# A dynamic-convolution block on one core: a new order of the first three images' work, a shorter coefficient chain, and the moments' gather one group earlier

## The reference, cut to what matters

```python
x0 = (x - mean) / sqrt(var + 1e-5)              # _gn: per image and channel
pooled = x0.mean(axis=(-2, -1))
gate = softmax(pooled @ gate_w.T + gate_b)      # (16, 7)
kw1 = einsum('be,eoihw->boihw', gate, experts_w1) + conv1_w   # kb1, kw2, kb2 likewise
out1 = relu(conv3x3_same(x0, kw1) + kb1)        # per image
out2 = conv3x3_same(out1, kw2) + kb2
result = x + x0 + out2
```

## Time and profile before

| | us |
|---|---|
| median of three runs | 357.04 |
| profiled execution | 357.09 |
| its span | 355.1 |
| TensorE busy | 308.5 |
| VectorE busy | 269.6 |
| ScalarE busy | 254.0 |
| GpSimd busy | 204.7 |

### The profile page before, as it was taken

One profiled execution on the slowest core, in us unless ns is written; L12 is line 12 of the kernel. 1 busy time (PEld: TensorE's weight loads), 2 busy tenths in 40 slices (PEclk: granted clock), 3 DMA queues, 4 the chain that ended last, 5 costly groups with the idle time before them and its releaser, 6 DMA issues.

```text
span 355.1 us, 7776 instructions
## 1 busy us (share of the span) xinstructions
PE 308.5 (87%) x3047; PEld 218.8 (62%) x3047; DVE 269.6 (76%) x571; ACT 254.0 (72%) x294; POOL 204.7 (58%) x240
## 2 busy tenths in 40 slices
PE   1416955499999998999899999999999989999994
PEld 2315743257767686777677677766776867655552
DVE  3699955588969798798879897989697978693432
ACT  1155229896969797898879797979697968866710
POOL 8038607593939485676749493949294947921000
PEclk9999969699999999999999999999999999999999
DMA  8942940599999799979998999999998993665055
GB/s 196 223 76 60 223 95 3 109 201 205 202 207 219 176 213 213 212 169 209 217 210 167 210 208 211 183 209 207 218 185 187 216 217 79 166 141 144 2 134 133
DMA packets 109380, 60.87 MB, mean 171 GB/s; under 512 B 102944, under 2 KB 105248, under 8 KB 109344
## 3 DMA queue, kind: packets, MB, share of 16 engines
q1 hardware_dynamic: 108544, 59.79, 80.8%
q10 hardware_dynamic: 608, 0.59, 0.6%
q0 software_dynamic: 192, 0.01, 0.0%
HBM read 19.47 MB, written 18.87 MB: 108 GB/s over the span
## 4 chain that ended last, share of the span: by engine, by line
PE 66%; DVE 18%; DMA 8%; ACT 3%; issue 3%; SPq 1%; ACTq 0%; DVEq 0%
PE pg L381 63%; DVE mix L649 7%; DMA wts<-wts 7%; DVE a L679 2%; DVE col L658 2%; PE pg L340 2%; DVE stats L607 2%; DMA natural<-in_L_conv_conv_w 1%; DVE wts L665 1%; SPq L297 1%; DVE wts L672 1%; PE pstat L361 1%; ACT xh L496 1%; ACT c L549 1%; ACT a L501 1%
## 5 line engine op out<-in xcount | busy, mean ns | idle before, releaser
L381 PE MATMUL pg<-a,wts 128*64 128x480 f16 (+1 forms) x1440 | 291.9, 363 | 11.5 <-DMA wts<-wts 6.1
L381 PE MATMUL pg<-c,wts 128*64 128x480 f16 (+1 forms) x1440 | 292.4, 367 | 0.0
L381 PEld LDWEIGHTS pg<-c,wts 128*64 128x64 f16 x1440 | 154.3, 110 | 49.4 <-issue 0.9
L381 PEld LDWEIGHTS pg<-a,wts 128*64 128x64 f16 x1440 | 155.0, 110 | 46.6 <-DMA wts<-wts 8.5
L539 ACT ACTIVATE hid<-pg,col 128x480 f32<-128x480 f32 x80 | 52.6, 658 | 45.2 <-PE pg L381 36.7
L869 POOL TENSOR_TENSOR a<-xh,a 128x576 f16<-128x576 f32 x64 | 79.0, 1271 | 4.4 <-issue 2.1
L549 ACT COPY c<-a 64x2352 f32<-64x2352 f32 (+2 forms) x48 | 71.9, 1497 | 2.3 <-DVE a L679 1.9
L850 POOL TENSOR_TENSOR col<-col,minus_half 128x1 f32<-128x1 f32 x16 | 13.8, 860 | 99.5 <-DVE col L622 99.5
L679 DVE TENSOR_TENSOR a<-hid,a 128x480 f16<-128x480 f32 x80 | 53.1, 665 | 22.6 <-ACT a L539 22.4
L649 DVE SCALAR_TENSOR_TENSOR mix<-bank,gate,mix 128x386 f32<-128x386 f32 x96 | 62.9, 655 | 2.4
L883 POOL TENSOR_SCALAR img<-img,col 128x1152 f32<-128x1152 f32 x32 | 64.6, 2025 | 0.1
(11 more groups left out here) (60 smaller groups left out, 140.9 us busy)
## 6 DMA issues: line engine op xcount, KB each, us to landing
c<-a SPq DMA_DIRECT2D x28, 588.0 KB, 6.5
img<-in_x SPq DMA_DIRECT2D x56, 288.0 KB, 7.0
out<-img SPq DMA_DIRECT2D x60, 180.0 KB, 3.1
out<-img SPq DMA_DIRECT2D x60, 108.0 KB, 2.4
wts<-wts SPq DMA_DIRECT2D x28, 96.0 KB, 3.2
c<-a SPq DMA_DIRECT2D x8, 294.0 KB, 5.2
img<-in_x SPq DMA_DIRECT2D x16, 144.0 KB, 5.0
out<-img SPq DMA_DIRECT2D x4, 120.0 KB, 2.1
```

The costliest lines, as they stand in the source:

```text
L381: last = nc.tensor.matmul(pg[g][side * 64:side * 64 + 64, at:at + nb * W].rearrange("p (b w) -> p b w", w=W), wts[s.c % WSETS][kind][:, v, ...
```

## The change

- **ScalarE** issues the loads of the first kernel set, then the six small rows (until now GpSimd's), then the second set. It copies kernel parts 0, 2, 4, 5, 6, 7, VectorE 1 and 3; parts 4 to 7 go through pg[4] and pset.
- **VectorE** takes image 0's statistics in two halves as soon as the first set is padded. mixture_first(v), weights_first(v) mix image 0's kernels by convolution, v = 0 first: seven operations on 193 columns each, then the same for v = 1 later. Image 1 and on are mixed whole. Only image 0's conv1 weights are crossed by VectorE; its conv2 weights and all of image 1's are crossed by DMA.
- **Images 0 and 1** do conv1 in two passes (early_conv1: HI with two products, LO with the third), with the normalised image made, lowered and crossed in halves. Gathers and logits of images 1 to 3 stand between these passes, and the orders of all engines are written out up to image 3's gather; slot starts at 2 (1 on GpSimd), with image 1's conv1 ahead of image 0's conv2 as before.
- **warm_up** has 8 matmuls instead of 7, behind the gather of image 1, and doesn't wait for weights.
- **hid** has four buffers instead of two; the two new ones lie in natural.
- **coefficients** has four operations instead of six: channel_moments also writes the difference OFF of partition and channel mean, from which gwp follows in one operation; the gate's product comes ahead of the normalisation's offset.
- **In every slot** the gather stands behind conv1's third group instead of its fourth, and softmax_in behind finish(2) instead of finish(1).

The core of the diff, with long deletions left out:

```diff
 EARLY = 2
-WARM = 7
+WARM = 8
...
+            def cross_weights_first():
...
+            load_early(first)
+            load_early(second)
+            load(third)
+            cross1_early(first, HI, 0)
+            cross1_early(first, HI, 1)
+            cross1_early(first, LO, 0)
+            cross1_early(second, HI, 0)
+            cross1_early(first, LO, 1)
+            cross1_early(second, HI, 1)
+            cross_weights_first()
+            load(fourth)
+            cross1_early(second, LO, 0)
+            cross_weights(second)
+            cross1_early(second, LO, 1)
...
             def warm_up():
-                pe.wait_ge(whi_ok, 1)
+                pe.wait_ge(wt_dve, 2)
                 for _ in range(WARM):
-                    nc.tensor.matmul(pset[:, P:2 * P], ident[:, :], same[:, :], start=True, stop=True)
+                    nc.tensor.matmul(pg[3][:, 0:P], ident[:, :], same[:, :], start=True, stop=True)
...
+            def early_conv1(s, g, part):
+                if part == HI:
+                    if g == 0:
+                        if s.known(0):
+                            pe.wait_ge(w_early, 1)
+                        else:
+                            pe.wait_ge(w_crossed[s.ring], 32)
+                        pe.wait_ge(crossed1_high[s.ring][0], 32)
+                    elif g == 2:
+                        pe.wait_ge(crossed1_high[s.ring][1], 32)
+                    if s.known(0):
...
+            transpose_kernels(0)
+            transpose_kernels(1)
...
+            transpose_kernels(2)
+            transpose_kernels(3)
+            gather_rows(first)
+            transpose_kernels(4)
+            transpose_kernels(5)
+            logits(first)
+            transpose_kernels(6)
+            transpose_kernels(7)
+            gather_rows(second)
...
+            early_conv1(first, 0, HI)
+            logits(second)
+            for g in range(1, GRP):
+                early_conv1(first, g, HI)
+            early_conv1(first, 0, LO)
+            early_conv1(first, 1, LO)
+            gather_rows(third)
+            early_conv1(first, 2, LO)
+            early_conv1(first, 3, LO)
+            early_conv1(first, 4, LO)
+            for g in range(GRP):
+                early_conv1(second, g, HI)
+            logits(third)
+            for g in range(GRP):
+                early_conv1(second, g, LO)
+            conv2_group(first, 0)
+            gather_rows(fourth)
+            conv2_group(first, 1)
+            conv2_group(first, 2)
+            conv2_group(first, 3)
+            logits(fourth)
+            conv2_group(first, 4)
...
                 run(conv1_group, s, 0, 2, 2)
+                run(gather_rows, s, 2, 4)
                 run(conv1_group, s, 0, 2, 3)
...
+            load_kernels(0)
+            load_rows()
+            load_kernels(1)
+            copy_kernels(0)
+            copy_kernels(2)
+            high_early(first, 0)
+            copy_kernels(4)
+            exponentials(first)
+            high_early(first, 1)
+            normalise_early(first, 0)
+            copy_kernels(5)
+            weights_high_first(0)
+            copy_kernels(6)
+            copy_kernels(7)
+            normalise_early(first, 1)
+            high_early(second, 0)
+            normalise_early(second, 0)
+            exponentials(second)
+            high_early(second, 1)
+            weights_high_first(1)
+            normalise_early(second, 1)
+            hidden(first, 0)
+            hidden(first, 1)
+            hidden(first, 2)
+            weights_high(second)
+            hidden(first, 3)
+            hidden(first, 4)
+            exponentials(third)
+            normalise(third)
+            high_part(third)
+            cross2(first, 0)
+            cross2(first, 1)
+            for g in range(GRP):
+                hidden(second, g)
+            weights_high(third)
+            cross2(second, 0)
+            cross2(second, 1)
+            normalise(fourth)
+            high_part(fourth)
+            exponentials(fourth)
...
+                nc.vector.tensor_tensor(c[:, OFF:OFF + 1], mv[t.ring][:, 0:1], c[:, MEAN:MEAN + 1], ALU.subtract)
...
+            def mixture_first(v):
+                t = Sample(0, 0)
+                dve.wait_ge(wt_act, 6 if v else 2)
+                dve.wait_ge(wt_dve, 2)
+                dve.wait_ge(table_ok, 1)
+                for e in range(E):
+                    if e > 0:
+                        dve.wait_ge(mix_step, (weight_sets(t, v) - 1) * (E - 1) + e)
+                    nc.vector.scalar_tensor_tensor(
+                        out=mix[:, (e + 1) % 2, v, :], in0=bank[:, e, v, :], scalar=gate[0][:, e:e + 1],
+                        in1=bank[:, E, v, :] if e == 0 else mix[:, e % 2, v, :],
+                        op0=ALU.mult, op1=ALU.add).then_inc(mix_step if e < E - 1 else mix_ok, 1)
...
+                low = nc.vector.tensor_tensor(st[:, v, LO, :], mix[:, E % 2, v, 0:TAPS], st[:, v, HI, :], ALU.subtract)
+                if v == 1:
+                    low.then_inc(w_first, 1)
+                    return
+                link(low)
+                for a, b in ((0, 1), (1, 0)):
+                    last = nc.vector.tensor_copy(halves(cr)[a][:, v].rearrange("p a b -> p (a b)"),
+                                                 halves(st)[b][:, v].rearrange("p a b -> p (a b)"))
+                last.then_inc(w_early, 1)
...
             row_constants()
             pad_kernels(0)
+            statistics_early(first, 0)
+            repeat_table()
+            statistics_early(first, 1)
+            aggregate(first)
             copy_kernels(1)
+            copy_table()
             copy_kernels(3)
+            channel_moments(first)
             pad_kernels(1)
+            statistics_early(second, 0)
+            softmax_in(first)
+            statistics_early(second, 1)
+            softmax_out(first)
+            mixture_first(0)
+            aggregate(second)
+            weights_first(0)
+            channel_moments(second)
+            mixture_first(1)
+            statistics(third)
+            softmax_in(second)
+            aggregate(third)
+            softmax_out(second)
+            weights_first(1)
+            channel_moments(third)
             for e in range(E):
+                mixture(second, e)
+            hidden_low(first, 0)
+            biases(second)
+            weights(second)
+            softmax_in(third)
+            hidden_low(first, 1)
+            hidden_low(first, 2)
+            hidden_low(first, 3)
+            hidden_low(first, 4)
+            clear_rim(first)
+            softmax_out(third)
+            mixture(third, 0)
+            statistics(fourth)
+            aggregate(fourth)
+            mixture(third, 1)
+            mixture(third, 2)
+            hidden_low(second, 0)
+            channel_moments(fourth)
+            mixture(third, 3)
+            hidden_low(second, 1)
+            mixture(third, 4)
+            hidden_low(second, 2)
+            mixture(third, 5)
+            hidden_low(second, 3)
+            mixture(third, 6)
+            hidden_low(second, 4)
+            clear_rim(second)
+            biases(third)
+            weights(third)
+            finish(first, 0)
+            finish(first, 1)
+            softmax_in(fourth)
+            finish(first, 2)
+            finish(first, 3)
...
                 run(finish, s, -1, 0, 1)
-                run(softmax_in, s, 2, 2)
                 run(finish, s, -1, 0, 2)
+                run(softmax_in, s, 2, 4)
                 run(finish, s, -1, 0, 3)
...
+                nc.gpsimd.tensor_scalar(gwp[t.ring][:, :], table[:, 0:E], c[:, OFF:OFF + 1], c[:, RSTD:RSTD + 1],
+                                        ALU.mult, ALU.mult).then_inc(gwp_ok, 1)
                 nc.gpsimd.tensor_scalar(c[:, NBIAS:NBIAS + 1], c[:, MEAN:MEAN + 1], c[:, RSTD:RSTD + 1], -1.0,
                                         ALU.mult, ALU.mult).then_inc(coef_ok, 1)
...
+                link(nc.gpsimd.tensor_scalar(c[:, RS1:RS1 + 1], c[:, RSTD:RSTD + 1], 1.0, None, ALU.add))
...
+            coefficients(first)
+            low_early(first, 0)
+            coefficients(second)
+            low_early(first, 1)
+            low_early(second, 0)
+            coefficients(third)
+            low_early(second, 1)
+            residual_bias(first)
+            residual(first)
```

More of the change, by code:

```diff
@@ L298, in cross_weights @@
                                  halves(st)[b].rearrange("p v a b -> p (v a b)")).then_inc(w_crossed[t.ring], 16)
[L300 to L305 removed]
+            def cross_weights_first():
+                sp.wait_ge(w_first, 1)
+                st, cr = wts[0][STRAIGHT], wts[0][CROSSED]
+                for a, b in ((0, 1), (1, 0)):
+                    sp.dma_start(halves(cr)[a][:, 1].rearrange("p a b -> p (a b)"),
+                                 halves(st)[b][:, 1].rearrange("p a b -> p (a b)")).then_inc(w_crossed[0], 16)
```

(32 more changed lines are left out.)

360 lines of the change are left out of this document (174 added, 186 removed).

## The result

The changed kernel takes 361.02 us in the median of four runs (360.82 to 363.28), the kernel before 357.13 beside it (356.76 to 357.82): ratio 1.012, 95% interval 1.008 to 1.016. It is slower, by 1.2%. The forecast was 358.6, with a range of 353.3 to 363.2 and slower as the likeliest sign. The profiled execution took 363.28 with a span of 361.5 and is the longest of its group; the others had spans of 359.0 to 359.6. In ten executions measured later one took 395.34 at a mean clock of 0.839, where the others took 358.42 to 361.29 at 0.964 to 0.966; no row is taken from it.

A forecast was written before the change was run, and what follows sets the result against it. The prediction took TensorE's work plus its gaps as the bound. From a span of 355.1 us, +6.1 for the beginning and -4.6 for the steady part gave 356.6, and 2.0 above the span gave 358.6; range 353.3 to 363.2.

The forecast's parts named there:

- slower as the likeliest sign: Whole kernel: a time more than 0.7 us above 357.04, chance 0.58.
- gain of the steady part: Later images: 4.6 us of weights waits taken back, of an estimated 5.5 behind image 3 (bounds 0 and 5.5).
- the 0.6 for the clock: Image 0's conv1, high pass: 0.6 us added for a clock not yet full (0 to 1.5).
- the first of my two readings: First mixing: a half operation waits for a whole GpSimd piece, about 1.45 us, rather than slowing in proportion, about 1.0.
- two terms too large: Image 1's weights: biases wait 1.3 us for GpSimd's residual; crossing by DMA takes 4.0 us to use.
- The logits: Image 2's logits, queued behind image 1's high pass, hold VectorE and ScalarE; 10.9 us from them to image 0's conv2.
- The gap of 8.6: TensorE's longest wait, ending at 67.1 before the change: not removed but moved, standing about 7.8 us before image 0's conv2.
- the step that failed: Image 3's conv1 needs no wait for weights; it starts at 104.8 against 98.67, so the beginning costs 6.1 us.
- the mechanism: Steady part: earlier stores let the image load start sooner, so weights behind it land at +18.0, inside a gapless 18.27 us.
- the likeliest case: Whole kernel: the forecast itself holds, 357.8 to 361 us, chance 0.43.
- Rival 1: Beginning works better: mixings don't collide (-2.1, -2.9), clock holds at image 2 (-1.2); 352.4 us, half 355.5; chance 0.27.
- Rival 4: Steady part gives nothing because DMA traffic sets the weights' landing; the 4.6 fall away, 363.2 us, slower; chance 0.15.

The follow-up runs named there:

- b_steady: The kernel before with the change's earlier gather, later softmax_in and short coefficients, but the old beginning: 354.33 us, ratio 0.990; a second time 353.78 us, 0.989.
- a_mix: The changed kernel with image 1's mixing, biases and weights ahead of channel_moments(third) and hidden_low(first, 0), and weights_high(second) ahead of hidden(first, 0): 359.37 us, ratio 1.004.
- a_logits: The changed kernel with logits(third) ahead of image 1's high pass instead of behind it: 349.40 us, ratio 0.975.
- a_l_high: a_logits with normalise(fourth) and high_part(fourth) ahead of cross2(second) on ScalarE: 346.61 us, ratio 0.969.
- a_best: a_l_high with a_mix's order, image 1's weights crossed by VectorE, and image 2 mixed in one piece earlier: 346.47 us, ratio 0.969.
- a_pool: The changed kernel with GpSimd's low_early(first, 0) put behind coefficients(second): 358.59 us, ratio 1.003.
- b_gather_finish: The kernel before with the gather one group earlier and softmax_in behind finish(2), without the short coefficients: 353.06 us, ratio 0.990.
- a_warm1: The changed kernel with one warm-up matmul instead of eight: 360.54 us, ratio 1.010.
- b_coef: The kernel before with the short coefficients alone: 368.55 us, ratio 1.028.

## Why the prediction was right, and where it wasn't

The marks, in the order of the forecast:

| | forecast | measured | before |
|---|---|---|---|
| image 0's mixing starts | 19.9 | 20.63 | |
| it lasts | 5.05 | 4.88 | |
| image 0's conv1 | 30.0 | 29.80 | 33.82 |
| image 1's weights ready | 47.5 | 45.3 | |
| image 1's conv1 | 51.5 | 48.69 | 48.3 |
| image 0's conv2 | 70.5 | 68.26 | 70.7 |
| image 2's conv1 | 85.3 | 83.43 | 79.67 |
| image 3's conv1 | 104.8 | 106.66 | 98.67 |
| gain of the steady part | 4.6 | 1.7 (3.8 in b_steady) | |
| span | 356.6 | 361.5 | 355.1 |

**The start: held, with a landing that wasn't in the sum.** The first mixing on VectorE beside GpSimd's low part and ScalarE's halves, and the row ahead of which the statistics waited:

```profile
11.98 1.48 DVE L719 BATCH_NORM_STATS2 stats<-img 128x6 f32<-128x384 f32 x3 [2.24 <-DMA img<-in_x]
...
20.63 0.42 DVE L783 SCALAR_TENSOR_TENSOR mix<-bank,gate 128x193 f32<-128x193 f32 x1
21.09 4.42 DVE L783 SCALAR_TENSOR_TENSOR mix<-bank,gate,mix 128x193 f32<-128x193 f32 x6
...
21.82 2.56 POOL L1021 TENSOR_TENSOR a<-xh,a 128x576 f16<-128x576 f32 x2 [4.60 <-ACT xh L570]
```

The second half of image 0 had landed by 11.98 in this execution, and by 9.5 to 10.4 in the profiles of the six experiments that share this start (forecast 10.5). There mixing starts at 18.1 to 19.0. This landing, 1.9 us later than theirs at the median, is most likely why the profiled execution is about 2 us longer than the others of its group, which have no trace of their own. It also makes image 0's conv1 at 29.80 look better forecast than it was: where the landing was early and the warm-up the same, conv1 started at 27.7 to 28.3 (a_mix, a_logits, a_l_high, a_best). Measured by those, the start was 1.2 us too late in my sum; the statistics, copies and small operations took 8.6 us from landing to mixing, not 9.4. The full clock at 29.80 is no rule either: in a_mix, a_logits and a_l_high conv1's first matmul took 0.53 instead of 0.35, so there the 0.6 for the clock was due. The small rows' new queue, put at nothing, has no run of its own; on ScalarE's queue their issues took 0.27 to 0.59 us each, on GpSimd's 0.51 to 0.76.

**The collision: the first of my two readings held.** Six operations took 4.42 us beside GpSimd's two pieces and 2.70 without them (a_pool), so a piece costs 0.86, and the two operations that met one took 1.30 and 1.29 in the chain: as long as a piece (2.56 / 2), not twice their own 0.45. The Trainium skill (SBUF — State Buffer, Who interferes with whom) says that the two engines hold the shared ports in turn for whole instructions; this row agrees, and so do image 1's two whole operations, 1.50 and 1.48 beside pieces of 3.11 / 2. I had 1.45 for a half operation; it is 1.30.

**Image 1's weights: two terms too large.** The biases took 0.15 and did not wait for the residual, for which I had 1.3: they ran from 44.70 although GpSimd's residual had started at 44.35. The crossing took 3.3 instead of 4.0. I had also named the wrong thing in front of them. VectorE's queue behind channel_moments(third) cost 0.44 us and not more, since the second half of image 0's kernels held it until 37.1, 1.12 us of that waiting for ScalarE's high part of these weights. And once it is shorter, as in a_mix, the load on SyncE's queue, 9.7 us ahead of the landing, is the limit, which I hadn't named for image 1. The clock over image 1's conv1 was 0.80 for 11.3 us, so 2.3 (forecast 2.0).

**The logits: held in place and size.** From VectorE's softmax_in to image 0's conv2 I had 10.9, and it was 68.26 - 57.28 = 11.0. a_logits shows that the cause is the order: 10.6 us with one line moved. The gap of 8.6 had moved and not gone, as forecast.

**Image 2: held.** Conv2 of image 0 to image 2's conv1 was forecast at 14.8 and took 15.2. The wait was 3.36, and the clock 0.75 from 84.70 to 90.00 (5.3 x 0.25 = 1.3; forecast 1.2), with another 0.4 in the 1.3 us ahead of that, at 0.68.

**Image 3: the step that failed.** "Image 3's conv1 needs no wait for weights, since the DMA queue had time" was the claim. It waited 3.2 us (PE busy for 0.47 us of the window of 3.60, with the DMA engines busy throughout), and the clock after it was 0.68 for 5.4 us, another 1.7. In a_pool the wait there was 2.9 and the clock stayed at 1.00, so this 1.7 isn't due each time. The chain of the last work ahead of it (start, duration, what):

```profile
81.70 2.31 ACT xh L570
84.01 2.21 ACT a L583
...
86.35 5.27 POOL a L1021 x4
...
91.64 0.63 SPq L301
...
92.97 2.59 SPq L274
...
101.39 1.28 SPq L324
...
102.71 3.90 DMA wts<-wts
```

ScalarE finished cross2(second) at 81.70, then normalised image 3, GpSimd made its low part, SyncE crossed it, and only then could the image load be issued: from 92.97, over 8.4 us, with the weights issued behind it at 101.39. Weights that VectorE had ready about 1 us earlier landed 13.7 us after the load's start, close to the 13.6 of the earlier trace rows. I had applied that row to the steady part and not here. The kernel before started the corresponding load at 85.02:

```profile
85.02 6.92 SPq L261 DMA_DIRECT2D img<-in_x  x4
```

I had followed TensorE's waits and not what a late cross2 does to the next image's load.

**The steady part: the mechanism held, the size didn't.** In b_steady it gives 3.8 of the forecast 4.6 in the trace and 3.4 to 3.5 in the medians, where b_gather_finish has 4.2, the gather's 2.0 and softmax_in's 2.2. The short coefficients, which I had as worth nothing, are worth nothing only beside the earlier gather: they take 0.92 us of VectorE's time in each slot, and alone they cost some 10 us. In the changed kernel TensorE's idle time over these ten images is 2.2 us in all, down from 5.4, which is the gain; but 1.7 us of low clock behind image 3's wait are in the same stretch, and 1.7 is left.

**The sum.** Forecast +6.1 - 4.6 = +1.5, measured +8.0 - 1.7 = +6.3 in the profiled execution. About 2 us of the 4.8 between them are the late landing, and 2.9 the steady part. Taken by the medians of the kernels measured together, the beginning cost 5.6 and the steady part gave 3.4: +2.2, near the forecast; by the first measurement it was +3.9, and 361.02 stands at the upper edge of the likeliest case. But this is partly luck. Without the late landing image 2's conv1 would stand near 81.5, 3.8 earlier than forecast, and image 3's near 104.8, right on it (an estimate, 1.9 off the rows above): the terms that were too large (1.2 at the start, 1.3 for the biases, 0.7 for the crossing) cover image 3's wait of 3.2, but not the 1.7 of low clock behind it, which weren't in the sum.

Rival 1 needed mixings without collisions and a clock kept over image 2's wait; the first mixing's collisions cost 1.7 and the clock 1.3. Rival 4 gave nearly the measured time of the profiled execution (363.2), but for a reason that b_steady excludes.

## What to carry to other kernels

When a kernel's beginning is rewritten by hand, follow each engine's list past the place where TensorE waits: here four tiny matmuls queued behind 60 others held VectorE for 12 us, ScalarE for 11 and then TensorE for 8, and moving them by one line turned a loss of 1% into a gain of 2.5%. A small transfer behind a large load on one queue landed with the load here, so ask when the load can be issued, and only then when the small data are ready. And a shortened chain on an engine that isn't critical must be costed too, by what its next work will run beside.

## What the runs showed of the hardware

- In these mixings a dependent VectorE operation that met a GpSimd piece took about the piece's time, whatever its own size: 1.30 us for 193 columns (0.45 alone) beside pieces of 1.28, 1.49 for 386 (0.65 alone) beside pieces of 1.55. So halving an operation didn't halve its price there.
- Where TensorE waited for it, the crossing of 192 KB of weights behind an image load landed 13.5 to 14.8 us after the load's start in seven kernels (before, changed, a_logits, a_l_high, a_best, a_mix, a_pool), with the weights issued 7.1 to 10.6 us after it; once, in a_warm1, it was 12.9. Early on, where the four load transfers were issued within 3 us instead of 7 to 8.4, it was 9.7 in a_mix, a_pool and a_warm1. That the load sets it, and not the weights, is read from these rows, a_best's above all; no run moved the load alone.
- Waits of 2.26 to 2.75 us were followed by the low clock in b_coef's steady part (0.66 for 5 us, 1.7 us each); waits of 2.03 and 2.10 in the same execution were not. The length of the wait alone doesn't tell: behind 2.82 us the clock was 0.66 in a_warm1 (at 88.49), behind 2.91 it was 1.00 in a_pool (at 102.93).
- Eight f32 warm-up matmuls took 3.37 us in the changed kernel and 3.44 in a_pool, and the first conv1 matmul behind them took 0.35; in a_mix, a_logits and a_l_high they took 3.78, and that matmul 0.53 (0.43 in a_best). At the end of the kernel no gain from them shows: 1.010 without (a_warm1), 1.007 and 1.012 with.
